# A two-sequence gated recurrence and ternary feed-forward layer on one core: x loaded by single tiles and its norm in halves, other places for a PSUM sum, a gate, one high part and one absolute sum

## The reference

```python
xn = (x - mean) / sqrt(var + 1e-5)                    # per token
# branch 1: gated linear recurrence, all weights 256 x 256
y    = gelu(xn @ w_y + b_y)
xb   = xn @ w_x + b_x
conv = conv_b + sum_k conv_w[k] * shift(xb, 3 - k)    # 4 taps along the tokens
gate_x = sigmoid(conv @ w_ig + b_ig);  gate_a = sigmoid(conv @ w_ag + b_ag)
log_a  = -8 * gate_a * softplus(a_param);  a = exp(log_a)   # a = 0 at token 0
nx = gate_x * conv * sqrt(1 - exp(2 * log_a))               # root = 1 at token 0
h[t] = a[t] * h[t-1] + nx[t]
out1 = (h * y) @ w_out + b_out
# branch 2: feed-forward, hidden size 682, weights made ternary with one scale each
wq   = clip(round(w / mean|w|), -1, 1) * mean|w|
out2 = (silu(xn @ w1q.T) * (xn @ w3q.T)) @ w2q.T
out  = x + out1 + out2
```

## Time and profile before

| | us |
|---|---|
| three runs | 78.19, 78.32, 381.07; median 78.32 |
| profiled execution, its own time | 78.11 |
| its span in the profile | 76.3 |
| TensorE matmul busy | 70.2 (92%) |
| VectorE busy | 62.0 (81%) |
| ScalarE busy | 49.9 (65%) |
| GpSimd busy | 31.8 (42%) |

### The profile page before, as it was taken

One profiled execution on the slowest core, in us unless ns is written; L12 is line 12 of the kernel. 1 busy time (PEld: TensorE's weight loads), 2 busy tenths in 40 slices (PEclk: granted clock), 3 DMA queues, 4 the chain that ended last, 5 costly groups with the idle time before them and its releaser, 6 DMA issues.

```text
span 76.3 us, 1057 instructions
## 1 busy us (share of the span) xinstructions
PE 70.2 (92%) x364; PEld 59.4 (78%) x364; DVE 62.0 (81%) x98; ACT 49.9 (65%) x76; POOL 31.8 (42%) x42
## 2 busy tenths in 40 slices
PE   4997999989998999999999999849999999999960
PEld 4995698858885678888888789648878888899950
DVE  4694999999999999999969999789999999400340
ACT  3483716998999999999989669994347419100000
POOL 6175674049563730070008958340007818910000
PEclk9999999999999999999999999999999999999999
DMA  0999999800000000000000000000000000340062
GB/s 4 285 253 370 377 402 388 282 11 0 0 0 0 4 0 0 0 0 0 5 0 0 9 0 0 0 0 0 0 0 0 0 0 0 108 167 9 0 206 69
DMA packets 5063, 5.63 MB, mean 74 GB/s; under 512 B 493, under 2 KB 4546, under 8 KB 5058
## 3 DMA queue, kind: packets, MB, share of 16 engines
q1 hardware_dynamic: 4914, 5.55, 21.3%
q10 hardware_dynamic: 144, 0.01, 0.1%
HBM read 4.51 MB, written 1.05 MB: 73 GB/s over the span
## 4 chain that ended last, share of the span: by engine, by line
PE 42%; DVE 29%; issue 10%; ACT 8%; DMA 4%; POOL 3%; ACTq 0%; DVEq 0%
PE slot L667 12%; PE slot L650 11%; PE slot L700 9%; PE slot L711 9%; DVE conv L493 9%; DVE xn_y L450 5%; DMA x_sb<-x 4%; DVE stats L437 4%; DVE xt_lo L456 3%; DVE w_raw L515 2%; ACT ta L363 2%; ACT L332 2%; POOL g_lo L257 2%; DVE w_raw L559 2%; ACT below L408 1%
## 5 line engine op out<-in xcount | busy, mean ns | idle before, releaser
L257 POOL TENSOR_TENSOR g_lo<-w_raw,g_hi 128x512 fp32r<-128x512 f32 x10 | 14.8, 1492 | 17.9 <-ACT g_hi L338 17.9
L667 PE MATMUL slot<-xt_lo,w_q 128*128 128x512 f32 x40 | 15.7, 394 | 0.0
L667 PE MATMUL slot<-xt_hi,w_q 128*128 128x512 f32 x40 | 15.7, 393 | 0.0
L700 PE MATMUL slot<-w_q,g_hi 128*128 128x256 f32 x40 | 10.2, 293 | 1.3 <-POOL g_lo L257 1.3
L332 ACT ACTIVATE w_raw<-slot,scale 128x512 f32<-128x512 f32 x10 | 6.8, 686 | 4.9 <-PE slot L667 4.9
L700 PE MATMUL slot<-w_q,g_lo 128*128 128x256 f32 x40 | 9.8, 282 | 0.0
L493 DVE SCALAR_TENSOR_TENSOR conv<-slot,par,conv 128x511 f32<-128x511 f32 (+2 forms) x12 | 9.0, 749 | 0.4
L700 PEld LDWEIGHTS slot<-w_q,g_hi 128*128 128x128 f32 x40 | 7.6, 191 | 1.8 <-POOL g_lo L257 1.7
L667 PEld LDWEIGHTS slot<-xt_lo,w_q 128*128 128x128 f32 x40 | 7.5, 188 | 1.7
L667 PEld LDWEIGHTS slot<-xt_hi,w_q 128*128 128x128 f32 x40 | 7.5, 188 | 1.7
L338 ACT ACTIVATE g_hi<-w_raw 128x512 fp32r<-128x512 f32 x10 | 6.3, 630 | 3.2 <-DVE w_raw L515 2.9
(11 more groups left out here) (105 smaller groups left out, 144.1 us busy)
## 6 DMA issues: line engine op xcount, KB each, us to landing
w_raw<-w13t SPq DMA_DIRECT2D x2, 682.0 KB, 7.6
w_raw<-dense SPq DMA_DIRECT2D x5, 256.0 KB, 5.8
out<-x_sb SPq DMA_DIRECT2D x3, 256.0 KB, 2.2
w_raw<-w2t SPq DMA_DIRECT2D x1, 640.0 KB
x_sb<-x SPq DMA_DIRECT2D x2, 256.0 KB, 3.0
x_sb<-x SPq DMA_DIRECT2D x1, 512.0 KB, 5.4
out<-x_sb SPq DMA_DIRECT2D x2, 128.0 KB, 1.7
w_raw<-w2t SPq DMA_DIRECT2D x2, 42.0 KB
```

The costliest lines, as they stand in the source:

```text
L257: nc.gpsimd.tensor_tensor(g_lo[:, j, s], g[:, n % RING], g_hi[:, j, s].bitcast(f32), ALU.subtract).then_inc(g_lo_set, 1)
L667: mm = nc.tensor.matmul(slot[H_SLOT[s][j]][:, o], w13_q[:, c, col:col + P], v[:, s, c], start=(c == 0 and v is xt_hi), stop=(c == KC - 1 a ...
L700: mm = nc.tensor.matmul(out_tile(s, i, t), v[:, s, rows], w2_q[:, j], start=(first and j == 0 and t == tiles.start and k == 0), stop=(not ...
```

## The change

Six places of the lists are altered; no arithmetic is.

- SyncE loads the first sequence of x in four DMAs of one tile instead of two of two tiles. They stand at the head of its queue, so that every later load is issued behind two more DMA instructions.
- The norm of the first sequence is made in two halves: statistics, aggregation and sum for tiles 0 and 1, then for tiles 2 and 3; GpSimd takes the power in two instructions of two numbers a partition; `normalise` waits for each.
- The first sequence's second gate goes to PSUM slot 0 instead of 3, the second sequence's first gate to slot 3 instead of 0. The sum of |w1| and |w3| no longer stands inside the first gate product but behind it. The second gate product of the first sequence now waits for the convolution of the second sequence (`conv_set`, the last reader of slot 0), no longer for the thresholds (`thr_set`).
- On ScalarE the absolute sum of w1 moves behind the high part of the second transposes, and the high part of w_ig ahead of them.
- On ScalarE the high part of the fifth hidden block moves ahead of the table load and the first root.
- The waits ahead of `hidden(1)` and `hidden_tail` follow the new slots.

```diff
-        GX_SLOT, GA_SLOT = (2, 0), (3, 1)
+        GX_SLOT, GA_SLOT = (2, 3), (0, 1)
...
-            for i in range(2):
-                t = slice(i * TILES // 2, (i + 1) * TILES // 2)
-                sp.dma_start(x_sb[:, 0, t], x_dram[0][:, t]).then_inc(x_loaded[i], 16)
+            for t in range(TILES):
+                sp.dma_start(x_sb[:, 0, t], x_dram[0][:, t]).then_inc(x_loaded[t], 16)
...
-            rstd_of(0)
+            rstd_of(0, slice(0, TILES // 2), 1)
+            rstd_of(0, slice(TILES // 2, TILES), 2)
             pool.wait_ge(xn_set, TILES)
             square_lo(WX)
-            rstd_of(1)
+            rstd_of(1, slice(0, TILES), 3)
...
+            tile_halves = (range(0, TILES // 2), range(TILES // 2, TILES))
             for i in range(2):
-                dve.wait_ge(x_loaded[i], 16)
-                statistics(0, range(i * TILES // 2, (i + 1) * TILES // 2))
-            variance(0)
-            normalise(0)
+                for t in tile_halves[i]:
+                    dve.wait_ge(x_loaded[t], 16)
+                    statistics(0, [t])
+                variance(0, tile_halves[i])
+            for i in range(2):
+                normalise(0, tile_halves[i], i + 1)
...
             pe.wait_ge(conv_set, KC)
-            gate_product(0, WIG, GX_SLOT, gx_psum, sums_of_w13)
+            gate_product(0, WIG, GX_SLOT, gx_psum)
+            sums_of_w13()
+            pe.wait_ge(conv_set, 2 * KC)
+            gate_product(0, WAG, GA_SLOT, ga_psum)
             pe.wait_ge(thr_set, 3)
-            gate_product(0, WAG, GA_SLOT, ga_psum)
-            pe.wait_ge(conv_set, 2 * KC)
             gate_product(1, WIG, GX_SLOT, gx_psum, sum_of_w2)
```

More of the change, by code:

```diff
@@ L135, in xt_bank @@
             return slot[T_SLOT[s]][:, h].rearrange("p (c n) -> p c n", c=KC)
-        x_loaded = [sem(f"x_loaded{i}") for i in range(3)]
+        x_loaded = [sem(f"x_loaded{i}") for i in range(TILES + 1)]
         w_loaded = [sem(f"w_loaded{m}") for m in range(5)]
@@ L227, in square_lo, with rstd_of @@
                 nc.gpsimd.tensor_tensor(w_lo[:, m], w_raw[:, m], w_hi[:, m].bitcast(f32), ALU.subtract).then_inc(w_lo_set, 1)
-            def rstd_of(s):
-                pool.wait_ge(v_set, s + 1)
+            def rstd_of(s, tiles, ready):
+                pool.wait_ge(v_set, ready)
                 pool.wait_ge(power_set, 1)
-                nc.gpsimd.tensor_tensor(rstd[:, s], v_eps[:, s], power[:, :], ALU.pow).then_inc(rstd_set, 1)
+                nc.gpsimd.tensor_tensor(rstd[:, s, tiles], v_eps[:, s, tiles], power[:, tiles], ALU.pow).then_inc(rstd_set, 1)
             def conv_constants():
@@ L375, in _ @@
             newest_tap(0)
+            square_hi(WIG)
+            xt_hi_of(1)
             act.wait_ge(w1_loaded, 16)
             abs_sum_of(w13_raw[:, :, 0:HIDDEN], KC, junk_a, 0, abs13_set)
-            xt_hi_of(1)
-            square_hi(WIG)
             square_hi(WAG)
@@ L415, in _ @@
             g_hi_of(3)
+            g_hi_of(4)
             mult_of(0, 0)
-            g_hi_of(4)
             mult_of(0, 1)
@@ L437, in statistics, with variance, normalise @@
                     nc.vector.bn_stats(stats[:, s, t], x_sb[:, s, t]).then_inc(stats_set, 1)
-            def variance(s):
-                for t in range(TILES):
+            def variance(s, tiles):
+                for t in tiles:
                     dve.wait_ge(stats_set, TILES * s + t + 1)
                     nc.vector.bn_aggr(mv[:, s, t], stats[:, s, t]).then_inc(mv_set, 1)
[L444 to L449, removed]
+                dve.wait_ge(mv_set, TILES * s + tiles.stop)
+                t = slice(tiles.start, tiles.stop)
+                nc.vector.tensor_scalar(v_eps[:, s, t], mv[:, s, t, 1], EPS, None, ALU.add).then_inc(v_set, 1)
+            def normalise(s, tiles, ready):
+                dve.wait_ge(rstd_set, ready)
+                for t in tiles:
                     nc.vector.tensor_scalar(xn[:, s, t], x_sb[:, s, t], mv[:, s, t, 0:1], rstd[:, s, t:t + 1],
@@ L574, in tail_lo @@
                                         gt_hi[HALF:HALF + TAIL].rearrange("p s n -> p (s n)").bitcast(f32), ALU.subtract).then_inc(gt_lo_set, 1)
+            tile_halves = (range(0, TILES // 2), range(TILES // 2, TILES))
             for i in range(2):
-                dve.wait_ge(x_loaded[i], 16)
-                statistics(0, range(i * TILES // 2, (i + 1) * TILES // 2))
-            variance(0)
-            normalise(0)
-            dve.wait_ge(x_loaded[2], 16)
+                for t in tile_halves[i]:
[4 more added lines that the diff above has]
+                normalise(0, tile_halves[i], i + 1)
+            dve.wait_ge(x_loaded[TILES], 16)
             statistics(1, range(TILES))
-            variance(1)
+            variance(1, range(TILES))
             xt_lo_of(0)
-            normalise(1)
+            normalise(1, range(TILES), 3)
             dve.wait_ge(sp_log, 1)
@@ L784, in _ @@
             hidden(0)
+            pe.wait_ge(ta_set, KC)
+            hidden(1)
             pe.wait_ge(tx_set, 2 * KC)
-            hidden(1)
-            pe.wait_ge(ta_set, KC)
             hidden_tail()
```

2 lines of the change are left out of this document (1 added, 1 removed).

## The result

The changed kernel takes **77.59 us** (median of 20 runs, 76.78 to 78.56) against 78.32 (median of 20, 78.16 to 381.07). The ratio is 0.9877, 95% interval 0.9859 to 0.9895: 0.96 us less, 0.82 to 1.10 by the interval. The profiled execution took 77.82 us, its span is 76.0 (before 78.11 and 76.3). Forecast were 77.8 and a gain of 0.5. So sign and range were right, and half of the gain was not seen.

What follows compares the result with a forecast made beforehand. It took VectorE's list to bound the kernel ahead of 25 us, and the chain of low parts TensorE near 50 us. Terms 0 - 0.2 - 0.3 = -0.5 took 78.11 to 77.6, median 77.8; range 76.7 to 78.9.

Steps and rivals of the forecast that it cites:

- x by tiles: First sequence's x load: an earlier first tile is worth nothing, and 0.4 us of slack covers the later second load; 0.
- The norm in halves: First sequence's norm: GpSimd's second power blocks VectorE, so normalising starts 0.1 us later; bounds 0.6 earlier and 0.9 later.
- doesn't block: Rival at the first norm: GpSimd's power does not block VectorE, norm 0.6 us earlier, 77.2 us; chance 0.08.
- Absolute sum and gates: Taps and second gate product: shorter small sum, TensorE 0.3 us earlier, ScalarE's chain gains 0.2 at most; -0.2 us.
- Fifth high part: Low parts near 48 us: GpSimd, VectorE, GpSimd take turns on the ports, TensorE resumes at 50.3, not 50.57; -0.3 us.
- GpSimd twice: Rival near 48 us: GpSimd makes two low parts in a row ahead of VectorE's, total 76.85 us; chance 0.10.
- the far bound of -1.25: Bound of the fifth high part's term: if GpSimd goes twice in a row, TensorE resumes at 49.3, -1.25 us.
- The race lost: Rival at 17.2 us: GpSimd's low part starts first, VectorE's small sum ends 0.8 us later, total 78.7 us; chance 0.25.

Runs made afterwards that it cites:

- either run with a fill: Changed kernel plus an unused VectorE fill just ahead of the second small sum for the taps: 256 numbers a partition, 77.25 us; 512 numbers, 77.64 us.
- the three kernels in which VectorE was held back: Changed kernel with VectorE's tail low part behind GpSimd's fifth: 77.34 us; also with sixth block's product earlier: 78.78 us; that with x by halves: 78.36 us.

## Why the prediction was right, and where it was off

The separate gains add up: -0.43 (norm in halves), -0.37 (gates, sum, absolute sum) and -0.27 (fifth high part) make -1.07, against -0.96 [-1.10, -0.82] for the whole. The forecast of -0.5 had no gain for the first of these, -0.2 for the second and -0.3 for the third. So the time came out inside the range with one mechanism of three wrong, and the range was wide enough to hold it.

- **x by tiles, 0:** right in sum, wrong in its reason. I had seen that an earlier first tile is worth nothing because GpSimd is not free before 5.51. In the profile after, GpSimd was free earlier (its constants end at 5.15 instead of 5.51; the parameters' landing also wanders), the first half was used and the norm ended 0.4 sooner than with halves. The later landing of the second x took it back: the 0.4 us of slack that I had counted was there only while the norm ended at 8.11, and its landing at 7.63 was an early one (7.6 to 8.2 with two loads ahead).
- **The norm in halves, +0.1: the step that failed.** (It has no term of its own in the sum; its 0.1 stands in the start of the second gate product.) "By that, the first tile waits for the second power" carried over to a power what a subtraction of 512 numbers did. All profiles with two powers show VectorE normalising through the second one. That the power of two numbers costs 0.73 to 0.84 instead of 0.62 lay inside the bounds. The rival "doesn't block", which I gave 0.08, was the right one, though its price of 0.6 came about otherwise than I had it. The norm itself is only 0.15 shorter, 2.31 against 2.46 from the start of the power, as its second half still waits for the second power. What else there is comes from a power that need not wait for the sum over all four tiles; I had that sum ready by 5.6, and in two of the three profiles with the old norm it held GpSimd until 5.9. The runs give 0.43 in all. The second x's landing takes about 0.1 of it in two of the three profiles with halves (7.92 and 7.96 behind a norm that ends at 7.83), and nothing in the third.
- **Absolute sum and gates, -0.2:** right in mechanism, small in size; it measured -0.37. The small sum took 0.15 as forecast, and the race went as forecast, by 0.05; VectorE's last tap came 0.34 sooner by it, for which I had taken 0.2. What I mis-sized is "the rest of its list hardly moves, so the chain behind it gains 0.2 at most". I read the gap of 0.17 as the most that ScalarE can gain there; without its wait the tanh came 0.26 sooner behind L349. And the list had moved by 0.11 ahead of it, from the newest tap on, where ScalarE no longer waits for TensorE. That is a part of the 0.45 that TensorE gains at the second transposes, which I had counted as nothing: it reached ScalarE before it was lost. The last tap has no share in the 0.11, since ScalarE has no printed gap between the newest tap and L349.
- **Fifth high part, -0.3:** right. Alone it measured -0.27, and TensorE resumed 42.20 behind the second statistics, before 42.55. The order of the three pieces on the ports came out both ways, with the same length (3.6). "GpSimd twice" ahead of VectorE also came about, in the three kernels in which VectorE was held back. In the one that changed nothing else it gave nothing: the far bound of -1.25 was no bound of this term, since TensorE meets the tail's low part next, and then VectorE's list, at 56.5.
- **The race lost (0.25):** its condition stood on 0.05 us, as written, but its price of 0.8 did not come about in either run with a fill, so it does not follow from who starts first alone. What the sum would do behind a low part's start without a fill ahead, at 0.05 or so, no run shows.

## What to carry to other kernels

Before a split or a move is charged with contention, look for a row of that very pair of instructions: a subtraction of 512 numbers (1.3 us) held VectorE up, and a power of two numbers (0.8 us) did not. An edit that frees a front end is worth only the time to the next landing, so look up the landing of the next load in more than one profile, and take it off before two executions are compared. A gap printed ahead of an instruction is not the most that its engine can gain there, as the engine's list ahead of it can move too. And where two engines share a port, moving one piece earlier changes who comes first everywhere behind it: here a product moved up by one instruction let a low part in ahead of a scan and cost the whole gain.

## What the runs showed of the hardware

- GpSimd's power takes 0.73 to 0.84 us for two numbers a partition and 1.00 to 1.04 for four, so doubling the count adds only 0.2 to 0.3; VectorE's normalising beside it runs at its own speed (0.41 for the first tile, as alone; the four take 1.54 against 1.38, as the third waits for the second power).
- The sum of two SBUF tensors 3 columns wide ran inside a GpSimd low part in 0.09 to 0.10 us behind a fill, and took 0.49 to 0.53 in the four profiles in which it came 0.8 us behind a low part's start without one.
- Two of ScalarE's instructions on 512 columns that follow each other without a wait overlap by about 0.1 us (32.90 + 1.24 against 34.04), so a wait between two such costs 0.1 more than the gap printed.
- The landing of one 512 KB load wandered between 7.8 and 8.5 us in seven profiles of kernels with the same loads ahead of it (two of them of the changed kernel), and moved what is behind it. Most of the spread of the changed kernel's runs (76.78 to 78.56) may be that; only profiled executions show where the load landed.
